# Experts ranked by token count on the chip, five of eight on gathered columns

## What is computed

```
logits = xf @ Wg                               # 256 x 8
top_w, top_i = top_k(logits, 2); top_w = softmax(top_w)
combine = einsum('nk,nke->ne', top_w, one_hot(top_i))
h = einsum('nc,ech->enh', xf, W1)              # 8 experts, 1024 hidden
g = einsum('nc,ech->enh', xf, W2)
y = einsum('enh,ehc->enc', silu(h) * g, W3)
out = einsum('enc,ne->nc', y, combine)         # x + out is returned
```

## Time and profile before

| | us |
|---|---|
| median of 3 runs | 1585.26 |
| lowest and highest | 1582.71, 1586.84 |
| span of the profiled execution | 1578.6 |
| PE busy | 1518.5 |
| VectorE (DVE) busy | 1311.8 |
| ScalarE (ACT) busy | 1266.7 |
| GpSimd (POOL) busy | 939.6 |

### The profile page before, as it was taken

One profiled execution on the slowest core, in us unless ns is written; L12 is line 12 of the kernel. 1 busy time (PEld: TensorE's weight loads), 2 busy tenths in 40 slices (PEclk: granted clock), 3 DMA queues, 4 the chain that ended last, 5 costly groups with the idle time before them and its releaser, 6 DMA issues.

```text
span 1578.6 us, 48054 instructions
## 1 busy us (share of the span) xinstructions
PE 1518.5 (96%) x17880; PEld 1254.2 (79%) x17880; DVE 1311.8 (83%) x1759; ACT 1266.7 (80%) x3054; POOL 939.6 (60%) x948
## 2 busy tenths in 40 slices
PE   6999999999999999999999999999999677999998
PEld 5788888888888888888888888888877555777776
DVE  7788888888888888888888888988888876767665
ACT  4888888888888888888888888888888765655554
POOL 5668787787877878778787787877866231000000
PEclk9999999999999999999999999999999787999999
DMA  4366655656566565665655656556565877655550
GB/s 180 75 137 115 138 115 135 139 114 136 114 137 139 113 137 114 135 140 113 139 113 133 144 109 140 120 125 146 108 135 110 171 174 238 216 203 197 209 203 25
DMA packets 460019, 220.24 MB, mean 140 GB/s; under 512 B 433840, under 2 KB 439984, under 8 KB 453184
## 3 DMA queue, kind: packets, MB, share of 16 engines
q1 hardware_dynamic: 459536, 218.22, 57.8%
q10 hardware_dynamic: 432, 1.32, 0.3%
HBM read 111.96 MB, written 0.56 MB: 71 GB/s over the span
## 4 chain that ended last, share of the span: by engine, by line
PE 88%; DVE 5%; DMA 2%; ACT 2%; POOL 1%; issue 1%; SPq 0%; POOLq 0%; DVEq 0%; ACTq 0%
PE ps_proj L1318 53%; PE ps_proj L1540 10%; PE ps_s L1368 9%; PE ps_o L1386 8%; PE ps_o L1563 5%; DMA pt_s<-p_s 2%; PE ps_proj L1347 1%; POOL ctx_s L421 1%; DVE cmax L948 1%; DVE wsp L1161 1%; DVE p_s L961 1%; DMA ctx_f<-ctxt_dram 1%; ACT prob L623 0%; PE ps_o L1288 0%; PE ps_o L1463 0%
## 5 line engine op out<-in xcount | busy, mean ns | idle before, releaser
L1318 PE MATMUL ps_proj<-ctx_s,wk_s 128*128 128x256 f16 x4032 | 480.6, 273 | 3.9 <-ACT ps_proj L577 3.6
L1318 PE MATMUL ps_proj<-wv_s,ctx_s 128*128 128x256 f16 x4032 | 480.6, 273 | 1.5 <-ACT ps_proj L579 1.5
L1318 PEld LDWEIGHTS ps_proj<-ctx_s,wk_s 128*128 128x128 f16 x4032 | 380.0, 98 | 66.4 <-issue 24.3
L421 POOL TENSOR_TENSOR ctx_s<-t_f,ctx_s 128x512 f16<-128x512 f32 x192 | 266.3, 1398 | 279.2 <-ACT ctx_s L525 279.2
L1318 PEld LDWEIGHTS ps_proj<-wv_s,ctx_s 128*128 128x128 f16 x4032 | 379.9, 98 | 63.5 <-issue 11.2
L623 ACT ACTIVATE prob<-ps_s,nmax 128x256 f32<-128x256 f32 x776 | 357.0, 476 | 8.0 <-DVE nmax L955 7.8
L948 DVE TENSOR_REDUCE cmax<-ps_s 128x4 f32<-128x1024 f32 x194 | 237.5, 1224 | 123.4 <-PE ps_s L1368 123.3
L961 DVE SCALAR_TENSOR_TENSOR p_s<-prob,p_s 128x1024 f16<-128x1024 f32 x196 | 321.2, 1639 | 0.7 <-ACT p_s L634 0.7
L421 POOL TENSOR_TENSOR ctx_s<-ctx_f,ctx_s 128x512 f16<-128x512 f32 x144 | 216.1, 1501 | 9.7 <-ACT ctx_s L520 4.8
L634 ACT ACTIVATE p_s<-prob 128x1024 f16<-128x1024 f32 x196 | 206.7, 1054 | 6.7
L1386 PE MATMUL ps_o<-v_s,pt_s 128*128 128x64 f16 x4704 | 172.2, 194 | 14.0 <-DMA pt_s<-p_s 14.0
(11 more groups left out here) (178 smaller groups left out, 1781.9 us busy)
## 6 DMA issues: line engine op xcount, KB each, us to landing
...
wst<-w_dram SPq DMA_DIRECT2D x96, 512.0 KB, 4.7
...
w_f<-wk_dram SPq DMA_DIRECT2D x2, 512.0 KB, 6.2
ctx_f<-ctxt_dram SPq DMA_DIRECT2D x2, 512.0 KB, 7.7
...
```

Of the source, the lines that this page charges most:

```text
L421: pool.tensor_tensor(out=low[:, n, :, :], in0=sources[n], in1=high[:, n, :, :], op=ALU.subtract).then_inc(ctx_low, 1)
L1318: ins = pe.matmul(ps_proj[:, bank(h, role), sub * QUARTER:(sub + 1) * QUARTER], lhsT, rhs, start=(fresh and sub == 0 and t == 0 and i == 0 ...
```

## The change

Expert 0 runs first, on all tokens. Meanwhile the other seven are ranked by their token counts: the chosen experts are counted over the tokens by a matmul with ones (`count`), VectorE compares the counts (`experts_by_rank`), and SP reads the expert of a rank from `whichi` into a register and loads its weights from a computed address. Rank j can hold at most 512 / (j + 1) tokens, so its columns are fixed when the program is built: 256, 256, 170, 128, 102, 86 and 74 (`CAPS`). `ORDER` gives the positions: expert 0, then ranks 0, 6, 2, 5, 3, 4, 1.

Ranks 0 and 1 run on all 256 tokens as before. The five others run on gathered columns, 560 in all: for each of six tiles of at most 128 slots, `picks` makes a selection matrix, `gather` multiplies both parts of xn by it into columns `xg_s` (in steps 8 to 13, beside rank 0), turns it for the way back (`place`) and gathers the tokens' weights (`wslot`). The output of such an expert is weighed and split in two parts (`y_s`, on ScalarE and VectorE) and spread back by 4 matmuls of 512 columns a tile that add up in `ps_s` (`scatter`); at step 45 VectorE adds the sum to `stream`.

With at most 128 columns a step holds the two blocks of a piece (48 matmuls, four steps an expert) and one output bank; rank 2 (170) keeps eight steps of 24 matmuls. In all 48 steps, written out, no loop. The split weights have four slots in place of two (`wsp2` in memory of the self-attention), and highs and remainders are made two pieces ahead. One remainder of the 96 is made by GpSimd (part 1 of piece 1, in two operations), 95 by VectorE as before. The routing comes before the first block. GpSimd makes the constants behind the cross-attention, and xn's float16 parts after the self-attention.

```diff
+CAPS = [min(T, (2 * T // (j + 1) + 1) // 2 * 2) for j in range(NR)]
...
+ORDER = (None, 0, 6, 2, 5, 3, 4, 1)
...
+def first_step(q):
+    return sum(NPC if not dense(i) and CAPS[ORDER[i]] <= P else 2 * NPC for i in range(q))
...
+def piece_of(n):
+    q = pos_of(n)
+    return NPC * q + (n - first_step(q)) // (1 if paired(q) else 2)
...
+        def on_pool(j, part):
+            return (j, part) == (1, 1)
...
+        def parts_of(n):
+            j = piece_of(n)
+            if n < 2:
+                return [(n + 1, p) for p in range(3)]
+            if j + AHEAD >= NJ:
+                return []
+            if paired(pos_of(n)):
+                return [(j + AHEAD, p) for p in range(3)]
+            return [(j + AHEAD, p) for p in ((0, 1), (2,))[(n - first_step(pos_of(n))) % 2]]
+        def low_parts_of(n):
...
-            with sp.Fori(4, NJ - 3, 4) as j:
-                for i in range(4):
-                    sp.wait_ge(piece_low, 3 * (j + (i - 3)))
-                    load_piece(j + i, i)
-            sp.wait_ge(combined, 2 * E)
+                load_piece(i)
+            sp.wait_ge(which_ready, 1)
+            for q in range(1, E):
+                expert = sp.value_load(whichi[0:1, ORDER[q]:ORDER[q] + 1], min_val=1, max_val=E - 1)
+                for i in range(NPC):
+                    old = NPC * (q - 1) + i
+                    sp.wait_ge(piece_low, lows_through(old, 2, False))
+                    if lows_through(old, 2, True):
+                        sp.wait_ge(piece_low_p, lows_through(old, 2, True))
+                    load_piece(i, expert * NPC + i)
+            sp.wait_ge(stream_step, 2 * sum(dense(q) for q in range(E)) + 2)
             sp.dma_start(out.rearrange("a (t r) d -> t (a r) d", r=2), stream[:, :, :]).then_inc(out_stored, 16)
...
+            pool.iota(ints[:, :], pattern=[[1, T]], base=1, channel_multiplier=0).then_inc(pool_step, 1)
+            pool.wait_ge(pool_step, 4)
+            pool.tensor_copy(iota1[:, :], ints[:, :]).then_inc(pool_step, 1)
+            pool.tensor_copy(ident_s[:, :], ident[:, :])
+            pool.memset(all_s[:, :], 1.0).then_inc(pool_step, 1)
+            pool.wait_ge(pool_step, 6)
+            pool.affine_select(out=earlier_s[:, :], in_=all_s[:, :], compare_op=ALU.is_ge, fill=0.0, base=-1,
+                               pattern=[[1, P]], channel_multiplier=-1)
+            for j in range(NR):
+                pool.memset(rank_c[:, j, :], float(j))
+            for e in range(E):
+                pool.memset(expert_c[:, :, e:e + 1], float(e))
+                ins = pool.memset(tie_c[:, e:e + 1], float(E - 1 - e) if e else -1e5)
+            ins.then_inc(const_ready, 1)
...
+            def piece_lows_p(j, n):
+                k = lows_through(j, n, True) - 1
+                pool.wait_ge(piece_loaded[j % 4], 48 * (j // 4) + 48)
+                if k >= 2:
+                    pool.wait_ge(piece_low_p, k - 1)
+                pool.tensor_scalar(wscaled[:, k % 2, :], wst[:, j % 4, n, :], FW_SCALE, None, ALU.mult).then_inc(scaled_p, 1)
+                pool.wait_ge(scaled_p, k + 1)
+                pool.wait_ge(piece_high, 3 * j + n + 1)
+                pool.tensor_tensor(out=weights(1, j)[:, n, :], in0=wscaled[:, k % 2, :], in1=weights(0, j)[:, n, :],
+                                   op=ALU.subtract).then_inc(piece_low_p, 1)
+            pool.wait_ge(ln_done, 6)
+            pool.tensor_copy(xt_s[0][:, :, :], xn[:, :, :]).then_inc(pool_step, 1)
+            pool.wait_ge(pool_step, 7)
+            pool.tensor_tensor(out=xt_s[1][:, :, :], in0=xn[:, :, :], in1=xt_s[0][:, :, :], op=ALU.subtract).then_inc(xt_done, 1)
+            for j in range(1, NJ):
...
+                if j >= SLOTS:
+                    if n < 2:
+                        act.wait_ge(hg_done, last_of_piece(j - SLOTS) + 1)
+                    else:
+                        act.wait_ge(y_done, last_of_piece(j - SLOTS) + 1)
+                act.activation(weights(0, j)[:, n, :], wst[:, j % 4, n, :], ACT.Copy, scale=FW_SCALE).then_inc(piece_high, 1)
...
+            def take_gathered(k):
+                q, o, w = RTILES[k]
+                at = gathered_at(q) + o
+                act.wait_ge(gathered, k + 1)
+                act.activation(xg_s[0][:, :, at:at + w], ps_proj[:, 2, :].rearrange("p (t c) -> p t c", t=DT)[:, :, 0:w], ACT.Copy)
+                act.activation(place[:, k, :], ps_s[:, 0, 0:T], ACT.Copy).then_inc(gat_high, 1)
...
+            def y_highs(q):
+                act.wait_ge(y_done, first_step(q + 1))
+                for i in range(row_tiles(q)):
+                    k = tile_of(q, i)
+                    if k >= 2:
+                        act.wait_ge(scattered, k - 1)
+                    act.activation(y_s[0][:, k % 2, :], ps_o[:, y_banks(q)[i], :], ACT.Copy,
+                                   scale=wslot[:, k:k + 1]).then_inc(y_high, 1)
...
+                if n == 1:
+                    experts_by_rank()
+                if n == 2:
+                    slots_by_rank()
+                if n == 3:
+                    picks(range(0, 3))
+                if n == 4:
+                    weigh()
+                    weights_by_rank()
+                if n == 5:
+                    picks(range(3, len(RTILES)))
+                if n == first_step(E - 1) + 5:
+                    take_scattered()
...
+            def gather(k):
+                q, o, w = RTILES[k]
+                if k == 0:
+                    pe.wait_ge(xt_done, 1)
+                    pe.wait_ge(weight_split, 1)
+                pe.wait_ge(picked, k + 1)
+                if k:
+                    pe.wait_ge(gat_high, k)
+                    pe.wait_ge(gat_low, k)
+                for a in range(2):
+                    for t in range(DT):
                         for r in range(2):
+                            pe.matmul(ps_proj[:, 2 + a, t * P:t * P + w], xt_s[a][:, r, t * P:(t + 1) * P], pick[:, k, r, 0:w],
+                                      start=(r == 0), stop=(r == 1))
+                for r in range(2):
+                    pe.matmul(ps_s[:, 0, r * P:(r + 1) * P], pick[:, k, r, :], ident_s[:, :], start=True, stop=True)
+                for i, (r, a) in enumerate(((0, 0), (0, 1), (1, 0), (1, 1))):
+                    ins = pe.matmul(ps_s[:, 1, 0:1], pick[:, k, r, :], comb_s[a][:, r, ORDER[q]:ORDER[q] + 1],
+                                    start=(i == 0), stop=(i == 3))
+                ins.then_inc(gathered, 1)
...
+            def hidden(n):
+                q, j = pos_of(n), piece_of(n)
+                w = columns(q)
+                pe.wait_ge(piece_low, lows_through(j, 1, False))
+                if lows_through(j, 1, True):
+                    pe.wait_ge(piece_low_p, lows_through(j, 1, True))
+                if n >= 2:
+                    pe.wait_ge(hh_done, n - 1)
+                if n == first_step(SPARSE[0]):
+                    pe.wait_ge(gat_high, len(RTILES))
+                    pe.wait_ge(gat_low, len(RTILES))
+                for m in range(2):
+                    for i, u in enumerate(units_of(n)):
+                        for t in range(DT):
                             for k, (a, b) in enumerate(THREE):
+                                col = t * PIECE + (u % 2) * P
+                                moving = x_s[b][:, t, :] if dense(q) else xg_s[b][:, t, gathered_at(q):gathered_at(q) + w]
+                                ins = pe.matmul(ps_proj[:, n % 2, m * T + i * P:m * T + i * P + w], weights(a, j)[:, m, col:col + P],
+                                                moving, start=(t == 0 and k == 0), stop=(t == DT - 1 and k == 2))
+                ins.then_inc(hg_done, 1)
...
+            def scatter(q):
+                for i in range(row_tiles(q)):
+                    k = tile_of(q, i)
+                    pe.wait_ge(combined, freed_through(q - 1) + i + 1)
+                    for r in range(2):
+                        for a in range(2):
+                            ins = pe.matmul(ps_s[:, r, :], place[:, k, r * P:(r + 1) * P], y_s[a][:, k % 2, :],
+                                            start=(k == 0 and a == 0), stop=(k == len(RTILES) - 1 and a == 1))
...
+            route()
+            for n in range(NSTEP + 2):
+                if n < NSTEP:
+                    hidden(n)
+                if n == 1:
+                    count()
+                if 0 <= n - first_step(1) < len(RTILES):
+                    gather(n - first_step(1))
+                if n >= 2:
+                    weigh3(n - 2)
+                for q in ends_at(n - 4):
+                    if not dense(q):
+                        scatter(q)
 
 
```

392 lines of the change are left out of this document (263 added, 129 removed).

## The result

The changed kernel takes 1530.88 us (median of 4 runs, 1528.73 to 1532.08), the kernel before in the same series 1584.78 (4 runs, 1582.71 to 1586.84). The ratio is 0.9659, 95% interval 0.9645 to 0.9674: 53.9 us less. The forecast was 1530, 1523 to 1550.

The account below looks back on a forecast made before the run. TensorE, busy 96% of the span, bounds the kernel, with VectorE next. Six stretches sum to 195.2 us against 252.7, 57.5 less; 2.5 taken back leaves 55, so span about 1523.6 plus 6.7 gives 1530, range 1523 to 1550.

Parts of the forecast that it names:

- hand-overs: Feed-forward stage: 2.5 us taken back for GpSimd beside VectorE at the start and output blocks waiting for their bank.
- Prices of TensorE: Matmul cost of 0.413 ns a column plus 3.4 ns, giving 34 ns for 74 columns, 56 for 128, 74 for 170.
- the first rival: Short matmuls stay at a 98 ns weight-load floor in the gathered experts: +37 us, 1567; chance 0.05.
- (a): Expert 0, eight steps with the routing ahead: 31.5 us, between 29.4 and 37, including a 2.1 us stall for GpSimd.
- the two-step lead of TensorE over hh just covers it: Expert 0: VectorE is full too, about 32 us plus some 2.5 of waits, yet should not delay TensorE.
- (b): Rank 0, dense, with six gathers beside it: 36.7 us, paced by TensorE.
- (f): Rank 1, dense, with one scatter and the last two output blocks: 34.8 us.
- (c): Rank 6, 74 columns, four steps: 16.8 us, bound by VectorE, where TensorE needs 11.7.
- (e): Ranks 5, 3 and 4, twelve steps: 50.1 us, bound by VectorE, where TensorE needs 46.
- (d): Rank 2, 170 columns, eight steps and one scatter: 25.3 us, bound by TensorE, where VectorE needs 18.2.
- the clock as a rival: Gathered experts: half clock in spells of 10 to 20 us, about 1545, chance 0.10; all through, 1604, chance 0.02.
- the 6.7 us "around the span": Whole kernel: median 1585.26 against profiled span 1578.6; the 6.7 us difference was to stay, added to span 1523.6.

Follow-up runs that it names:

- e14_silu: e12_best with the gate's exponential replaced by silu, sparing ScalarE two table loads; 1527.4 us, ratio 0.9640.
- e12_best: Changed kernel with single parts behind hh and banks, four output banks, no remainder on GpSimd, picks and weights moved partly later; 1526.6 us, ratio 0.9648.
- e3: Changed kernel with VectorE's remainders for the five gathered experts made on 512 of 1024 columns; 1522.8 us, ratio 0.9614.
- e6: Changed kernel with the columns of ranks 3 to 6 cut to 32 each; 1523.85 us, ratio 0.9633.
- e4: Changed kernel with the paired experts' outputs in two PSUM banks of their own; 1528.7 us, ratio 0.9652.
- after: The changed kernel itself, against the kernel before; 1530.88 us, ratio 0.9659.
- e5: Changed kernel loading half of each weight part for the ranked experts, in as many transfers; 1528.5 us, ratio 0.9658.
- e1_dense: Changed kernel with all seven ranked experts on all 256 tokens, no gathering or scattering; 1594.45 us, ratio 1.0073.

## Why the prediction was right, point by point

The time was right to 1 us; the sum behind it was 195.2 for the stage plus 2.5 for hand-overs, and 199.7 was measured. The mechanism held: fewer columns pay until VectorE's remainders, which do not shrink, set the pace.

*Prices of TensorE: right.* Groups of 48 take 1.63 us at 74 columns, 1.86 at 86, 2.16 at 102, 2.68 at 128, and 24 of 170 take 1.76 (start to start), as the line of 0.413 ns a column and 3.4 ns from the earlier trace rows gives. The floor of the first rival (98 ns from the earlier trace rows) is out, and so is the 81 ns for 128 columns of the Trainium skill (TensorE: Matmul & The Clock Gate, Back-to-back issue gap): 48 loads and matmuls at 128 columns in 2.68 us are 56 ns a pair.

*(a), 31.5 predicted, 34.1 measured: the mis-sized term.* Block 2's wait was 2.39 for a predicted 2.1, though GpSimd's four operations took 1.04, 2.13, 2.79 and 2.18 us and not 2.13 each: the errors cancel. The step that failed is "the two-step lead of TensorE over hh just covers it": block 7 waited 1.88. ScalarE's two table loads, 2.56 us that the sum did not list at all, are about half of such a wait (e14_silu, on e12_best's code: 1.97 to 0.98); what the other half is stays open, with VectorE's queue the likely cause. The prediction's terms for VectorE add up to 31.1 and not to "about 32", which changes nothing here. The text had named blocks 5 to 9 and an upper bound of 37.

*(b), (f): right* to 0.2. *(c) and (e), 66.9 predicted, 64.6 measured: right*, VectorE bounds them (e3, e6, e4). They came 2.3 lower because VectorE enters (c) with a lead: the first three hidden groups of (c) start 2.91 us apart, TensorE's own pace, and the wait comes only behind them. VectorE's lateness from (c) then shows in (d) as well, in the wait for y_s.

*(d), 25.3 predicted, 29.4 measured: wrong by 4.1.* The output group waited 2.22 for rank 6's y_s, and 1.7 more went to the half clock behind it. With its own banks it took 25.3. The prediction had both, the wait as "output blocks waiting for their bank" within 2.5 us taken back, the clock as a rival with 10 to 20 us; it cost 1.7 us, about a tenth of that.

*The sum against the time.* The 2.5 us were too few (4.5 needed). But the 6.7 us "around the span" did not carry over: 1529.2 is after's span, 1530.9 its median. In every run on record a time is only 1.7 to 1.8 us above its span; the other 5 us of the 6.7 were that the profiled execution of before was faster than the median of its kernel. The two errors, 2.0 in the stage and 3.3 in the stage's start against 5 around the span, cancel; the match to 1 us is luck, the match to some 5 us is not.

*Costs put at zero: right.* GpSimd's constants took 2.9 us (1265.92 to 1268.77) and its first remainder came after 16.05 us of idle time instead of 18.59. Loads: e5. Transfers landed in 5.8 us instead of 4.7, without effect.

*The signs it named.* VectorE's idle time in (c) and (e) is 1.5 us each, near zero as said. Expert 1 begins at 1358.9 and not near 1353: 3.3 us are this execution's later start, 2.6 are (a). "The clock shows 0.5 in the sparse steps", a sign of being wrong, did come, for 3 us in after and for 6 in e6_narrow; it was too short to decide the time.

*Missed altogether:* the order of the single part in odd steps. It costs 1 us at each end of a dense expert that another dense one follows. In after two such ends have a group behind them: expert 0's, where the gathers give VectorE the time (no wait stands there), and rank 0's, where VectorE is the bound anyway. So it costs 7 us in e1_dense and, as far as these rows show, nothing in after; no run puts the old order back into after alone.
